# Second layer of a two-layer transformer with expert networks: the chosen experts' output bias, fetched per token by indirect transfers and added on VectorE

## The chip, the cores and the metric

The kernel runs on 1 core of one Trainium2 chip. Its time is the device time of one execution in microseconds (us). Before the change the median of three runs is 465.22 us (464.97 to 474.35).

The engines are named as the profile names them: PE is TensorE (matrix products, with PEld for its weight loads), DVE is VectorE, ACT is ScalarE, POOL is GpSimd and SP is SyncE. PE writes its results to PSUM (`ps`), the other tiles lie in SBUF, and inputs and outputs in DRAM.

## What is computed

32 images become 50 tokens of 192 numbers each (49 patches and a class token). Two layers follow. Layer 0 is a gated linear recurrence and an expert network with two chosen experts out of eight. Layer 1 is an attention on complex queries and keys and a switch network, in which each token goes to one expert. The change lies in this last part:

```python
x_enc = xt @ enc_w + enc_b
route_prob = jax.nn.softmax(x_enc @ sw_w + sw_b, axis=-1)
route_prob_max = jnp.max(route_prob, axis=-1)
routes = jnp.argmax(route_prob, axis=-1)
onehot = jax.nn.one_hot(routes, E, dtype=xt.dtype)
h = jnp.einsum('td,edr->ter', xt, w1) + b1[None]
h = jax.nn.gelu(h, approximate=False)
h = h * onehot[..., None]
out = jnp.einsum('ter,erd->td', h, w2) + onehot @ b2
out = out * route_prob_max[:, None]
```

Here `xt` is the normed token, E is 8, and `b2` has a row of 192 numbers for each expert. The result is added to the token `h`.

## The kernel before

**Tiles and stages.** The 32 images are four chunks (`CHUNKS`) of eight images. A chunk holds 400 tokens as four tiles (`TILES`) of 128 rows, two images a tile, each image padded from 50 to 64 rows. Layer 0's attention part runs in pairs of tiles until about 115 us of the span, its experts in a loop over 32 expert tiles until about 270 us, and layer 1 fills the rest, some 185 us.

**Layer 1.** Every engine runs a list of instructions written out by hand. A loop over the chunk number c sets the order. Iteration c computes the attention of chunk c and, between its pieces, the switch network of chunk c-1. The switch network of chunk 3 stands behind the loop. On PE an iteration is: the transposes of chunk c-1 (`turn`, L674), then `scores` (L941) of the four tiles, with `encode` (L983), `switch_logits` (L991), `hidden` (L1007) and `turned_choice` (L999) of chunk c-1 in between; then the queries and keys of the next chunk (L909), then `outputs` of chunk c-1 (L1019, L1020), then `attention` (transposes of the weights L964, products L974), and the rest of the next chunk's queries, keys and values (L909, L920). In iteration 3 there is no next chunk: only half of `outputs(2)` stands ahead of `attention(3)`, the other half behind it, and then the transposes of chunk 3 (L1080) open the tail.

**The switch network's output.** `outputs(c, half)` multiplies, for each of two tiles, the hidden values `s_hidT` with `s_w2` in four products (L1019) and adds the bias in a fifth (L1020). The fifth one's operands are rows 96 to 103 of `xT[1]`, in which the one-hot choice of each token stands transposed, and `s_b2`, whose rows 0 to 95 are zero and whose rows 96 to 103 are `b2`. DVE then computes in `output(c, half)` (L1869 to L1885) `out_tok = ps * s_prob + h` for each tile. Its first part reduces the exponentials to `s_prob`; that waits for ACT's exponential (L1286), which ACT issues between the attention weights of tiles 0 and 1 (L1262).

**The choice.** `route(c)` on DVE (L1845 to L1867) reads the logits and makes `s_best` and `s_onehot`. It runs early in iteration c+1, behind the first tile's `add_squares` (L1787, L1790); `output(c, ...)` runs late in it, ahead of `context` (L1805, L1808, L1813, L1816), which scales the attention's result, adds it to `h` and takes the statistics. POOL computes the inverse deviations of the norms (`rooted`, L605 and L607), for which DVE waits before it writes the normed tokens (L1420, and L1832 for chunk 3). In the attention and expert parts of layer 0 POOL also issues indirect transfers: `scatter` (L623) and the stores of L649.

The functions in their own words:

## Time and profile before

| | |
|---|---|
| median of the runs | 465.22 us (464.97, 465.22, 474.35) |
| the profiled execution's time | 459.67 us |
| its span, first to last instruction | 457.9 us |
| PE busy | 417.6 us, 91% of the span |
| PEld busy | 366.1 us, 80% |
| DVE busy | 274.3 us, 60% |
| ACT busy | 204.0 us, 45% |
| POOL busy | 96.3 us, 21% |
| granted TensorE clock, mean | 0.976 |
| the chain that ended last, by engine | PE 71%, DVE 10%, ACT 7%, issue 4%, DMA 4%, POOL 2% |

The profile is of one execution. Busy times are sums over the span; engines overlap. The chain is followed back from the last instruction, at each step to what released it. In the timeline a row is an instruction or a run of like ones, with its start, its length and, in brackets, how long the engine had been idle and what ended that. A multiplication of 32-bit numbers on PE leaves two records for each product of the program, so that 16 bias products give 32 records. The granted clock is 1.00 (2.4 GHz) nearly everywhere in layer 1.

### The profile page before, as it was taken

What the parts mean: (1) busy time and instruction counts of PE and PEld (TensorE: products, weight loads), DVE (VectorE), ACT (ScalarE), POOL (GpSimd) and SP (SyncE); (2) the same over time, 40 slices, a digit from 0 to 9 for tenths busy, and PEclk for the clock granted to TensorE, in tenths of its full rate; (3) what the DMA queues carried; (4) which work ended last, traced back from release to release, by engine and by line L of the source; (5) the groups of instructions that cost most, each with busy time, mean ns of one, the idle gap of its engine ahead of it and who ended that gap; (6) DMA issues with size and microseconds to landing.
All of it is one profiled execution on the core that took longest, in us unless ns stands there. A gap on an engine that the chain in (4) does not pass through costs nothing.

```text
span 457.9 us, 11718 instructions
## 1 busy us (share of the span) xinstructions
PE 417.6 (91%) x3944; PEld 366.1 (80%) x3945; DVE 274.3 (60%) x992; ACT 204.0 (45%) x427; POOL 96.3 (21%) x139
## 2 busy tenths in 40 slices
PE   5999999987699999999999938988799999999986
PEld 5899999887599999999999937656559757777845
DVE  4478888876334544554554447977686673665621
ACT  1333334521134544543553431267585377368440
POOL 3113555555402113112212211110101100100100
PEclk9999999997699999999999988999999999999999
DMA  7899802411312112112212225200001000100010
GB/s 233 319 375 400 326 31 75 132 36 51 97 38 61 40 41 63 41 36 53 67 35 52 62 53 179 69 4 1 1 1 28 2 3 2 28 1 1 2 28 27
DMA packets 30082, 35.43 MB, mean 77 GB/s; under 512 B 9315, under 2 KB 25379, under 8 KB 30047
## 3 DMA queue, kind: packets, MB, share of 16 engines
q1 hardware_dynamic: 25115, 28.52, 19.5%
q0 software_dynamic: 3072, 4.95, 3.3%
q10 hardware_dynamic: 1860, 1.49, 1.1%
q8 instruction: 22, 0.36, 0.3%
q14 instruction: 13, 0.11, 0.1%
HBM read 27.19 MB, written 9.14 MB: 79 GB/s over the span
## 4 chain that ended last, share of the span: by engine, by line
PE 71%; DVE 10%; ACT 7%; issue 4%; DMA 4%; POOL 2%; SPq 1%; DVEq 1%; POOLq 0%; ACTq 0%
PE ps L883 13%; PE ps L851 8%; PE ps L698 7%; PE ps L909 6%; PE ps L1019 5%; PE ps L862 5%; PE ps L1007 4%; PE ps L941 2%; PE ps L974 2%; PE ps L742 2%; PE ps L964 2%; PE ps L752 1%; ACT squares L1249 1%; PE ps L983 1%; PE ps L920 1%
## 5 line engine op out<-in xcount | busy, mean ns | idle before, releaser
L883 PE MATMUL ps<-w,hidT 128*128 x384 | 65.1, 326 | 0.0
L883 PEld LDWEIGHTS ps<-w,hidT 128*128 128x128 f32 x384 | 62.0, 190 | 0.0
L649 POOL DMA_INDIRECT ys_dram<-ys,y_place_now x32 | 31.1, 972 | 117.3 <-DVE ys L1699 112.4
L1212 ACT ACTIVATE hidT<-ps,b_act_now 128x128 f32<-128x128 f32 x96 | 28.2, 364 | 51.5 <-issue 49.2
L851 PE MATMUL ps<-xsT,low_now 128*128 128x128 f32 x384 | 49.8, 280 | 0.1
L851 PEld LDWEIGHTS ps<-xsT,low_now 128*128 128x128 f32 x384 | 46.0, 191 | 2.4 <-ACT xsT L1188 0.4
L605 POOL TENSOR_TENSOR rstd<-meanvar,eps 128x2 f32<-128x2 f32 (+1 forms) x25 | 5.4, 216 | 187.5 <-DVE meanvar L1839 73.8
L1684 DVE TENSOR_SCALAR hidT<-ps,b_dve_now 128x128 f32<-128x128 f32 x96 | 27.7, 344 | 21.4 <-PE ps L862 21.4
L698 PE MATMUL ps<-w_tok,patches 128*128 128x192 f32 x192 | 36.0, 342 | 5.0 <-DMA patches<-in_patches 5.0
L685 PE MATMUL ps<-ident 128*128 128x128 f32 x164 | 27.5, 335 | 12.5 <-DMA y_first<-ys_dram 8.4
L623 POOL DMA_INDIRECT xs_dram<-x_tok,rows x32 | 32.0, 1001 | 28.0 <-DVE rows L1568 20.7
L698 PEld LDWEIGHTS ps<-w_tok,patches 128*128 128x128 f32 x192 | 33.5, 200 | 4.8 <-DMA patches<-in_patches 4.7
L685 PEld LDWEIGHTS ps<-ident 128*128 128x128 f32 x164 | 26.0, 246 | 13.3 <-issue 13.0
L1195 ACT COPY low_now<-w_low 128x768 f32 x34 | 28.3, 832 | 0.0
L862 PE MATMUL ps<-xsT,high_now 64*128 64x128 f32 x384 | 25.7, 280 | 0.0
L1007 PE MATMUL ps<-xT,s_w 96*128 96x400 f32 (+1 forms) x64 | 24.2, 512 | 1.6 <-ACT xT L1291 1.6
L1019 PE MATMUL ps<-s_w,s_hidT 128*128 128x192 f32 x128 | 23.9, 330 | 1.2 <-ACT s_hidT L1299 1.2
L862 PEld LDWEIGHTS ps<-xsT,high_now 64*128 64x128 f32 x384 | 22.7, 187 | 1.9
L1674 DVE COPY b_dve_now<-b 128x3 f32 x32 | 5.4, 169 | 30.5 <-DVE hidT L1684 27.0
L1019 PEld LDWEIGHTS ps<-s_w,s_hidT 128*128 128x128 f32 x128 | 21.0, 189 | 3.4 <-ACT s_hidT L1299 3.3
L1249 ACT ACTIVATE squares<-ps 128x1200 f32<-128x1200 f32 x16 | 18.7, 1171 | 9.4 <-PE ps L941 9.3
L1699 DVE TENSOR_TENSOR ys<-ps,b 128x192 f32<-128x192 f32 x32 | 11.4, 357 | 18.0 <-PE ps L883 9.9
(225 smaller groups left out, 787.8 us busy)
## 6 DMA issues: line engine op xcount, KB each, us to landing
patches<-in_patches SPq DMA_DIRECT2D x7, 768.0 KB, 7.7
w<-in_W SPq DMA_DIRECT2D x8, 576.0 KB, 11.9
xs<-xs_dram SPq DMA_DIRECT2D x36, 96.0 KB
w_low<-in_W_low SPq DMA_DIRECT2D x8, 384.0 KB, 11.1
w_high<-in_W_high SPq DMA_DIRECT2D x8, 192.0 KB, 11.3
y_first<-ys_dram SPq DMA_DIRECT2D x4, 384.0 KB, 3.7
y_second<-ys_dram SPq DMA_DIRECT2D x4, 384.0 KB, 4.4
xs<-xs_dram SPq DMA_DIRECT2D x36, 33.0 KB
```

The lines of the kernel that those rows point to most:

```text
L623: nc.gpsimd.indirect_dma_start(out=xs_dram[:, :], out_offset=bass.IndirectOffsetOnAxis(ap=rows[:, k, 2 * c + i:2 * c + i + 1], axis=0), in ...
L649: nc.gpsimd.indirect_dma_start(out=ys_dram[:, :], out_offset=bass.IndirectOffsetOnAxis(ap=y_place_now[v][:, 0:1], axis=0), in_=ys[v][:, :] ...
L685: pe.matmul(ps[:, bank, 0:P], ident[:, :], ident[:, :], start=True, stop=True)
L698: mm = pe.matmul(ps[:, c % 2, D * i:D * i + D], pair_of(patches, c)[:, i, k, :], w_tok[:, k, :], start=(k == 0), stop=(k == KC - 1))
L851: mm = pe.matmul(ps[:, 4 + 2 * v + m // 3, P * (m % 3):P * (m % 3) + P], low_now[v][:, P * m:P * m + P], xsT[v][:, 0, :], start=(starts an ...
L862: mm = pe.matmul(ps[:, 4 + 2 * v + half, P * j:P * j + P], high_now[v][rows_, P * j:P * j + P], xsT[v][rows_, 1, :], start=(starts and j = ...
L883: mm = pe.matmul(ps[:, 2 * v + 1, 0:D], hidT[v][:, m, :], w2[:, bass.ds(experts[v], 1), D * m:D * m + D].rearrange("p e n -> p (e n)"), st ...
L1007: mm = pe.matmul(ps[:, FFN[c][m], 0:CT], s_w1[0:k, g, P * m:P * m + P], seqs(xT[1][0:k, g, :]), start=(g == 0), stop=(g == 1))
L1019: pe.matmul(dst, s_hidT[:, m, P * i:P * i + P], s_w2[:, m, :], start=(m == 0), stop=False)
L1195: nc.scalar.copy(low_now[v][:, :], w1_low[:, bass.ds(e, 1), :].rearrange("p e n -> p (e n)")).then_inc(w1_act_done, 1)
L1212: last = nc.scalar.activation(hidT[v][:, m, :], ps[:, 4 + 2 * v, P * m:P * m + P], ACT.Relu, bias=b1_act_now[v][:, m:m + 1])
L1684: last = nc.vector.tensor_scalar(hidT[v][:, 3 + m, :], ps[:, 5 + 2 * v, P * m:P * m + P], b1_dve_now[v][:, m:m + 1], 0.0, ALU.add, ALU.max)
```

## The change

For chunks 0, 1 and 2 the fifth product (L1020) is left out, and the fourth one ends the accumulation. Chunk 3 keeps it. In its place:

- `route(c)` computes on DVE, behind `s_onehot`, the number of the bias row of each token, `bias_row = 104 - s_best`, as an integer (one instruction on 128x4).
- `load_biases(c)` on POOL waits for it (and for the previous use of the buffer) and issues four indirect transfers, one a tile. Each fetches for 128 tokens the row of 192 numbers (768 bytes) from the input `s_b2` in DRAM into the new tile `bias_tok`.
- `output(c, 0)` on DVE waits for the four transfers, computes `out_tok = bias_tok * s_prob + h` for all four tiles, waits for its own last write, and then adds `ps * s_prob` to `out_tok` where it used to add it to `h`.

```diff
--- before.py
+++ after.py
@@ -254,6 +254,8 @@
         s_rank = sb("s_rank", [P, TILES, E])
         s_best = sb("s_best", [P, TILES])
         s_onehot = sb("s_onehot", [P, TILES, E])
+        bias_row = sb("bias_row", [P, TILES], I32)
+        bias_tok = sb("bias_tok", [P, TILES, D])
 
 
 
@@ -353,6 +355,9 @@
         s_rank_done = sem("s_rank_done")
         s_best_done = sem("s_best_done")
         onehot_done = sem("onehot_done")
+        bias_row_done = sem("bias_row_done")
+        bias_in = sem("bias_in")
+        bias_added = sem("bias_added")
         onehotT_in_psum = sem("onehotT_in_psum")
         onehotT_done = sem("onehotT_done")
         s_hid_in_psum = sem("s_hid_in_psum")
@@ -656,10 +661,24 @@
 
                 for c in range(2):
                     inverse_deviation(2, c)
+                def load_biases(c):
+
+                    pool.wait_ge(bias_row_done, c + 1)
+                    if c:
+                        pool.wait_ge(bias_added, c)
+                    for i in range(TILES):
+                        nc.gpsimd.indirect_dma_start(
+                            out=bias_tok[:, i, :], out_offset=None, in_=A["s_b2"][:, :],
+                            in_offset=bass.IndirectOffsetOnAxis(ap=bias_row[:, i:i + 1], axis=0),
+                            bounds_check=FG + E - 1, oob_is_err=False).then_inc(bias_in, 16)
+
                 for c in range(CHUNKS - 1):
+                    if c:
+                        load_biases(c - 1)
                     if c + 2 < CHUNKS:
                         inverse_deviation(2, c + 2)
                     inverse_deviation(3, c)
+                load_biases(CHUNKS - 2)
                 for half in range(2):
                     of = slice(2 * half, 2 * half + 2)
                     rooted(meanvar[1][:, of, 1], rstd[1][:, of], CHUNKS + half, var_done[3], eps_added[3], rstd_done[3])
@@ -1016,9 +1035,11 @@
                     for i in range(2 * half, 2 * half + 2):
                         dst = tokv(4)[:, i // 2, i % 2, :]
                         for m in range(4):
-                            pe.matmul(dst, s_hidT[:, m, P * i:P * i + P], s_w2[:, m, :], start=(m == 0), stop=False)
-                        mm = pe.matmul(dst, xT[1][0:FG + E, 1, P * i:P * i + P], s_b2[:, :],
-                                       start=False, stop=True)
+                            mm = pe.matmul(dst, s_hidT[:, m, P * i:P * i + P], s_w2[:, m, :], start=(m == 0),
+                                           stop=(c < CHUNKS - 1 and m == 3))
+                        if c == CHUNKS - 1:
+                            mm = pe.matmul(dst, xT[1][0:FG + E, 1, P * i:P * i + P], s_b2[:, :],
+                                           start=False, stop=True)
                     mm.then_inc(s_out_in_psum, 1)
 
                 turn(2, 0, 0, 1)
@@ -1865,6 +1886,11 @@
                         dve.wait_ge(onehotT_in_psum, c)
                     nc.vector.tensor_tensor(s_onehot[:, :, :], s_rank[:, :, :], spread(s_best[:, :], E),
                                             ALU.is_equal).then_inc(onehot_done, 1)
+                    if n < CHUNKS:
+                        if c:
+                            dve.wait_ge(bias_in, 16 * TILES * c)
+                        nc.vector.tensor_scalar(bias_row[:, :], s_best[:, :], -1.0, float(FG + E), ALU.mult,
+                                                ALU.add).then_inc(bias_row_done, 1)
 
                 def output(c, half):
 
@@ -1876,11 +1902,19 @@
                         dve.wait_ge(s_prob_done, c + 1)
                         if c >= 2:
                             dve.wait_ge(out_done[c % 2], 32 * (c // 2))
+                        if c < CHUNKS - 1:
+                            dve.wait_ge(bias_in, 16 * TILES * (c + 1))
+                            for i in range(TILES):
+                                last = nc.vector.scalar_tensor_tensor(
+                                    out_tok[c % 2][:, i, :], bias_tok[:, i, :], s_prob[:, i:i + 1],
+                                    h_tile(c, i), ALU.mult, ALU.add)
+                            last.then_inc(bias_added, 1)
+                            dve.wait_ge(bias_added, c + 1)
                     dve.wait_ge(s_out_in_psum, 2 * c + half + 1)
                     for i in range(2 * half, 2 * half + 2):
                         last = nc.vector.scalar_tensor_tensor(
                             out_tok[c % 2][:, i, :], tokv(4)[:, i // 2, i % 2, :], s_prob[:, i:i + 1],
-                            h_tile(c, i), ALU.mult, ALU.add)
+                            out_tok[c % 2][:, i, :] if c < CHUNKS - 1 else h_tile(c, i), ALU.mult, ALU.add)
                     if half or c == CHUNKS - 1:
                         last.then_inc(out_ready, 1)
 
```

On PE, the end of iteration 3 and the switch network's output of chunks 2 and 3. `s_hidT`, `s_w_202`, `s_b_203` and `xT_86` are the tiles `s_hidT`, `s_w2`, `s_b2` and `xT[1]`. Before:

```order
L1019 MATMUL ps<-s_w_202,s_hidT 128x192 x4
L1020 MATMUL ps<-s_b_203,xT_86 128x192
L1019 MATMUL ps<-s_w_202,s_hidT 128x192 x4
L1020 MATMUL ps<-s_b_203,xT_86 128x192
L1080 MATMUL ps<-ident,x_tok_84 96x128 x8
L983 MATMUL ps<-xT_86,enc_w 64x400 x2
```

After:

```order
L1038 MATMUL ps<-s_w_202,s_hidT 128x192 x8
L1101 MATMUL ps<-ident,x_tok_84 96x128 x8
L1002 MATMUL ps<-xT_86,enc_w 64x400 x2
```

The bias products are gone, nothing took their place on PE, and the transposes of chunk 3 follow directly. The same holds for all twelve tiles of chunks 0 to 2.

On DVE, in iteration 2 of layer 1, from the output of chunk 1 to the first tile of the attention's result. `ctx_tok` is the scaled result of a tile. Before:

```order
L1873 TENSOR_REDUCE s_sum<-s_exp 128x4
L1875 RECIPROCAL s_prob<-s_sum 128x4
L1881 SCALAR_TENSOR_TENSOR out_tok_206<-ps,s_prob,h 128x192 x4
L1805 RECIPROCAL inv_sum_236<-ps 128x12
L1808 TENSOR_TENSOR ctx_tok_238<-ps,inv_sum_236 128x4x3x16
```

After:

```order
L1899 TENSOR_REDUCE s_sum<-s_exp 128x4
L1901 RECIPROCAL s_prob<-s_sum 128x4
L1908 SCALAR_TENSOR_TENSOR out_tok_206<-bias_tok,s_prob,h 128x192 x4
L1915 SCALAR_TENSOR_TENSOR out_tok_206<-ps,s_prob,out_tok_206 128x192 x4
L1826 RECIPROCAL inv_sum_236<-ps 128x12
L1829 TENSOR_TENSOR ctx_tok_238<-ps,inv_sum_236 128x4x3x16
```

Four instructions stand between `s_prob` and the first output, and `context` is behind them.

On POOL, from iteration 1 of layer 1 to its end, with the changed kernel's line numbers. `meanvar_75` and `rstd_79` belong to the norm ahead of the attention, `meanvar_76` and `rstd_80` to the one behind it.

```order
L670 DMA bias_tok<-in_s_b,bias_row 128x192 x4
L610 TENSOR_TENSOR rstd_79<-meanvar_75,eps 128x4
L612 TENSOR_TENSOR rstd_79<-rstd_79,neg_half 128x4
L610 TENSOR_TENSOR rstd_80<-meanvar_76,eps 128x4
L612 TENSOR_TENSOR rstd_80<-rstd_80,neg_half 128x4
L670 DMA bias_tok<-in_s_b,bias_row 128x192 x4
L610 TENSOR_TENSOR rstd_80<-meanvar_76,eps 128x4
L612 TENSOR_TENSOR rstd_80<-rstd_80,neg_half 128x4
L670 DMA bias_tok<-in_s_b,bias_row 128x192 x4
L610 TENSOR_TENSOR rstd_80<-meanvar_76,eps 128x2
L612 TENSOR_TENSOR rstd_80<-rstd_80,neg_half 128x2
```

Each group of four transfers now stands ahead of the inverse deviations that come later in its iteration.

## Rows read from the trace of the kernel before

**Rows 1.** Windows, iterations 1 and 3: length, busy us and records of each engine, clock
```profile
340.00:360.00 20.00, 19.54 (x180) 15.62 (x179) 14.35 (x50) 10.77 (x17) 2.41 (x4) 1.00 0.06 17
420.00:440.00 20.00, 18.90 (x192) 15.76 (x191) 8.54 (x30) 9.89 (x17) 1.84 (x4) 1.00 0.06 17
```

**Rows 2.** Chain that ended last, iteration 1, outputs of chunk 0: start, us, what
```profile
342.77 1.57 PE ps L1019 x8
344.34 0.33 PE ps L1020 x2
344.66 1.30 PE ps L1019 x8
...
349.22 0.33 PE ps L1020 x2
```

**Rows 3.** Timeline of DVE, iteration 1: start, us, instruction, idle before
```profile
330.94 0.19 DVE L1866 TENSOR_TENSOR s_onehot<-s_rank,s_best 128x32 f32<-128x32 f32 x1
...
334.19 0.78 DVE L1787 TENSOR_TENSOR sc<-squares 128x600 f32<-128x600 f32 x1 [0.86 <-ACT squares L1249]
...
347.73 0.18 DVE L1875 RECIPROCAL s_prob<-s_sum 128x4 f32<-128x4 f32 x1
347.94 0.74 DVE L1881 SCALAR_TENSOR_TENSOR out_tok<-ps,s_prob,h 128x192 f32<-128x192 f32 x2
...
352.03 0.23 DVE L1805 RECIPROCAL inv_sum<-ps 128x12 f32<-128x12 f32 x1 [1.71 <-PE ps L974]
...
353.66 0.23 DVE L1805 RECIPROCAL inv_sum<-ps 128x12 f32<-128x12 f32 x1 [0.22 <-PE ps L974]
```

**Rows 4.** Groups by line, DVE, 340 to 345 us: us of all, mean ns
```profile
L1738 DVE SCALAR_TENSOR_TENSOR h<-y_first,all_gates,h 128x192 f32<-128x192 f32 x4 | 1.4, 409 | 0.0
```

**Rows 5.** Timeline of DVE, iteration 2
```profile
370.68 0.19 DVE L1866 TENSOR_TENSOR s_onehot<-s_rank,s_best 128x32 f32<-128x32 f32 x1
...
385.33 0.18 DVE L1875 RECIPROCAL s_prob<-s_sum 128x4 f32<-128x4 f32 x1
...
391.78 0.23 DVE L1805 RECIPROCAL inv_sum<-ps 128x12 f32<-128x12 f32 x1 [1.71 <-PE ps L974]
```

**Rows 6.** Timeline of DVE, iteration 3
```profile
410.43 0.19 DVE L1866 TENSOR_TENSOR s_onehot<-s_rank,s_best 128x32 f32<-128x32 f32 x1
...
423.82 0.18 DVE L1875 RECIPROCAL s_prob<-s_sum 128x4 f32<-128x4 f32 x1
...
427.49 0.23 DVE L1805 RECIPROCAL inv_sum<-ps 128x12 f32<-128x12 f32 x1 [1.59 <-PE ps L974]
...
434.97 0.67 DVE L1832 TENSOR_SCALAR x_tok<-h,meanvar,rstd 128x192 f32<-128x192 f32 x2 [0.66 <-POOL rstd L607]
```

**Rows 7.** Timeline of ACT, iteration 3
```profile
423.47 1.88 ACT L1262 ACTIVATE sc<-sc 128x600 f32<-128x600 f32 x3
425.70 1.50 ACT L1270 COPY probsT<-ps 128x768 f32<-128x768 f32 x2 [0.35 <-PE ps L964]
```

**Rows 8.** Chain that ended last, iteration 3, transposes of chunk 3
```profile
435.11 0.91 PE ps L1080 x7
```

**Rows 9.** Line 623, POOL's indirect transfers of layer 0: ns and landing us, min/median/max
```profile
L623 POOL DMA_INDIRECT xs_dram<-x_tok,rows x32: 967/972/1213, 43.6 to 116.3; - x32
...
DMA to landing us min/median/max: 2.3/2.4/5.9
```

**Rows 10.** Timeline of POOL, layer 0
```profile
77.81 0.97 POOL L623 DMA_INDIRECT xs_dram<-x_tok,rows  x1 [0.30 <-issue]
```

**Rows 11.** DMA issues: KB each, median us to landing
```profile
w<-in_W SPq DMA_DIRECT2D x8, 576.0 KB, 11.9
```

**Rows 12.** Timeline of POOL, iteration 1: the two inverse deviations behind the first gathers
```profile
344.95 0.20 POOL L605 TENSOR_TENSOR rstd<-meanvar,eps 128x4 f32<-128x4 f32 x1 [21.63 <-DVE meanvar L1413]
```

**Rows 13.** Line 1467 on DVE, both inputs in SBUF: ns min/median/max
```profile
L1467 DVE TENSOR_TENSOR h_plus_x<-h_plus_x,x_tok x8: 529/546/600, 15.8 to 87.9; 128x384 f32<-128x384 f32 x8
```

**Rows 14.** Timeline of DVE, layer 0
```profile
77.79 0.60 DVE L1467 TENSOR_TENSOR h_plus_x<-h_plus_x,x_tok 128x384 f32<-128x384 f32 x1
```

## The prediction

> **What bounds the kernel now.** The windows come first: in two windows of 20 us that cover most of iterations 1 and 3 of layer 1, PE is busy 19.54 and 18.90 us, DVE 14.35 and 8.54, POOL 2.41 and 1.84, all at a granted clock of 1.00 [rows 1]. So PE sets the pace of this stage and POOL is nearly free. Then the chain of waits, to see whether the removed products lie on it: at the outputs of chunk 0 it is an unbroken run of PE, 1.30 us of L1019 and 0.33 us of L1020 in turn, for four tiles [rows 2]. The bias products are on the chain, and what they cost is their full length. Last the timelines of DVE and ACT around the same place, which show who is next when PE becomes shorter: DVE has waits of 1.71, 1.71 and 1.59 us in front of the first tile of the attention's result [rows 3, 5, 6], and ACT in iteration 3 has only 0.35 us in front of its copy of the first weights [rows 7].
>
> **What is removed: 12 bias products on PE.** Each takes 0.33 us (two records) [rows 2]. In iterations 1 and 2 four are taken out of an unbroken run: 4 x 0.33 = 1.3 us each. In iteration 3 two go ahead of the attention and two behind it, 0.66 + 0.66 us, but there two other engines are next:
> - Ahead of the attention. The copy of the first weights on ACT starts at 425.70 after a wait of 0.35 us, because ACT finishes the three exponentials of tiles 1 to 3 at 423.47 + 1.88 = 425.35 [rows 7]. ACT does not move with PE, so the start of this copy gains 0.35 us, or up to 0.45 us because the records of like ACT instructions overlap by some 0.1 us (three in 1.88 us). I take 0.4; 0.26 of the 0.66 is lost.
> - Behind the attention. From its second tile on DVE works without a pause: it ends with the normed tokens of tiles 2 and 3 at 434.97 + 0.67 = 435.64 [rows 6], and the transposes of chunk 3 end on the chain at 435.11 + 0.91 = 436.02 [rows 8]. This DVE chain is set off by the attention's second tile and so moves by 0.4 us only, to 435.24. The last tile's two transposes (of eight in 0.91 us, so about 0.25) with some 0.15 us of hand-over then end near 435.65. So nothing of the second 0.66 us arrives, and PE waits instead, some 0.6 us. Iteration 3 gives 0.4 us in all.
>
> Sum of the gains: 1.3 + 1.3 + 0.4 = 3.0 us, out of the 3.9 us of PE time removed.
>
> **What is added on POOL: 12 gathers.** The trace has no gather from DRAM into SBUF. The nearest rows are the indirect transfers of layer 0, also 128 rows of about this size: 0.97 us of POOL each and 0.30 us between two, so four take 3 x 1.27 + 0.97 = 4.8 us, and they land 2.4 us after the issue, at worst 5.9 [rows 9, 10]. The upper bound of a landing is the slowest row of any issue, 11.9 us [rows 11]; the lower one is 2.3. I take 2.4. Then the fourth gather is there 7.2 us after the row numbers. Row numbers at the end of `s_onehot` plus 0.2 us for the new small instruction: 331.3, 371.1 and 410.8. Needed when `s_prob` is done: 347.9, 385.5 and 424.0 [rows 3, 5, 6]. Spare: 9.4, 7.2 and 6.0 us. The gathers cost nothing as long as this cover holds. Queued behind them on POOL are the inverse deviations. In iteration 1 the first is asked for at 344.95 [rows 12], and POOL is free at 336.1. In iterations 2 and 3 they come later still, behind `context`. SP's queue is not passed. The 512 rows of a chunk are 0.4 MB, for a DMA that moves 17 GB/s here [rows 1].
>
> **What is added on DVE.** Per chunk one small instruction behind `s_onehot`, 0.2 us like its neighbours. It pushes the second `add_squares` by 0.2 us, and the wait of 0.86 us on ACT that follows takes it up [rows 3]; without that cover it would cost 0.6 us in all. Then four instructions on 128x192. The nearest row is the same instruction with all tensors in SBUF, four in 1.4 us [rows 4]. With the wait for its own write (0.05 us, taken as the gap between other dependent DVE instructions of rows 3) it is 1.45 us. Without cover that would be 4.35 us in all, which is more than the PE time removed. The cover is DVE's wait ahead of `context`, and it must hold although PE comes earlier:
> - Iteration 1: start 347.94, bias until 349.4, four outputs (two in 0.74 us, four in 1.4) until 350.8. The attention's first tile is there at 352.03 - 1.3 = 350.7. DVE is 0.1 us late, and the wait of 0.22 us in front of the next tile absorbs it [rows 3].
> - Iteration 2: start 385.5, bias until 387.0, the last outputs follow PE until some 388.8; needed at 391.78 - 1.3 = 390.5 [rows 5].
> - Iteration 3: start 424.0, bias until 425.5, two outputs until 426.2; needed at 427.49 - 0.4 = 427.1 [rows 6].
>
> So DVE costs 0 to 0.1 us. The sum stays 3.0 us. The profiled execution has a span of 457.9 us and a time of 459.67 us. It would become 454.9 and 456.7. The median of the runs shown lies 5.5 us above the profiled execution; the same 3.0 us off it gives 465.2 - 3.0 = 462.2 us.
>
> **A rule that speaks against the change.** When an indirect transfer ran beside a DVE instruction with two inputs in SBUF, POOL's part kept its 0.97 us and DVE's took 0.60 us where the median of its line is 0.546 [rows 10, 13, 14]. So I charge nothing for it; at 0.05 us for each of some five DVE instructions beside the gathers it is 0.25 us an iteration, under the waits of 0.86 us. The Trainium skill, SBUF — State Buffer, section "Who interferes with whom", says otherwise: a DVE instruction with two SBUF inputs and a GpSimd instruction that reads SBUF exclude each other for their whole length, and the one that starts second is held. By that rule the gathers and DVE's `add_squares` and shifts, which have both inputs in SBUF, would hold each other; this is the third rival.
>
> **Rivals.**
> 1. *The last iteration gives its whole 1.3 us* (0.08). For it: the chain passes PE there. Against: the two waits above of 0.35 and 0.66 us. It gives 465.2 - 3.9 = 461.3.
> 2. *The gathers come late; slower than before* (0.07). All 512 fetches of a chunk read the same eight rows of DRAM, which nothing in this trace does. Place: DVE's wait in `output(c, 0)`, with `context` queued behind it and PE's last attention products behind that. In iteration 3 it bites when the landing exceeds 2.4 + 6.0 + 0.9 = 9.3 us, in iteration 2 from about 11.7, in iteration 1 from about 11.8, and it decides the sign from about 12.3. At 12.5 the second tile of iteration 3 is 2.5 us later than before, iteration 2 keeps a gain of about 1.0 and iteration 1 of 0.7: +0.8, 466.0. At 16 us it would be some 11 us slower, over 2%.
> 3. *POOL and DVE hold each other; slower than before* (0.07). Beside four gathers of 0.97 us DVE runs some five long instructions. If each gather held DVE for its length, that is 3.9 us an iteration, less the wait of 0.86: 3.0, three times 9.1, less the gain of 3.0: 465.2 + 6.1 = 471.3. Half of it would be 466.8. Against: rows 13 and 14, which show 0.05.
> 4. *DVE is late for `context`* (0.10). If the added instructions or the wait for the own write cost 0.3 us more than taken, iteration 1 uses up its wait of 0.22 and passes the rest on, some 0.2 us, and iteration 3 is near its limit too; if the misjudgement is 1 us, about 0.8 us is lost: 463.
>
> **How the numbers follow.** The forecast has 0.68, its own range from 461.3 to 463.2 us. The rivals' 0.08, 0.07, 0.07 and 0.10 make it 1.00. The range takes in rivals 1 and 4 and the near end of 2, and below that the level of the runs themselves: the profiled execution of the same kernel was 5.5 us under the median, so a median that falls in between is possible. That gives 459.0 to 466.0. Only rival 3 and the far end of 2 are left out, and the runs' own scatter. Over 2% (9.3 us, about what a measurement of this kernel can tell from no change) faster needs more than twice the PE time that is removed: 0.01. Over 2% slower needs the far end of rival 2, or 2 and 3 together (6.1 us alone is 1.3%): 0.03. Within 2%: 0.96.
>
> **What would show it.** In the changed profile: 12 fewer bias products (24 records), iteration pitch on PE shorter by 1.3, 1.3 and 0.4 us; the gathers of 0.97 us with landings near 2.4 us, 6 us ahead of their use; `s_prob` followed at once by the four additions in about 1.4 us; `context` in iteration 1 with no wait in front of its first tile; in iteration 3 ACT's copy with no wait in front, and the transposes L1101 now waiting some 0.6 us for DVE's `x_tok`. Wrong it would be if DVE waits for `bias_tok`, if the `sc` instructions beside the gathers are longer than 0.8 us, or if the clock falls below 1.00 in layer 1.

## The result and the profile after

The changed kernel takes 486.06 us (483.24 to 492.27, six runs) where the kernel before takes 465.1 us (461.49 to 474.35, six runs): 1.046 times as long, interval 1.0384 to 1.0537. It is 21 us slower, and the forecast was 3 us faster. The profiled execution took 485.37 us; its span is 483.6 us. Any kernel has executions that are some per cent slower at a lower clock; ratios leave these out, so a ratio can differ a little from the quotient of two medians.

The chip matters in this case, so each run below is told with the number of its chip (that of the first measurement is not known). The page of the kernel before shows a chip of one kind, the page after one of another: line 1233 (ACT's `hidT` in layer 0's experts; line 1212 before) waits 53.3 us in all for "issue" after, and 49.2 us before, although the change does not touch it. DVE's first sum of layer 1 (line 1738 before, 1759 after) starts at 281.10 instead of 275.65. These 5.5 us lie ahead of everything that was changed. What the change does is therefore read from the stage itself, from one `s_onehot` to the next; this distance is called the pitch of an iteration (start us, us, instruction):

```profile
338.12 0.19 DVE L1887 TENSOR_TENSOR s_onehot<-s_rank,s_best 128x32 f32<-128x32 f32 x1
...
383.65 0.19 DVE L1887 TENSOR_TENSOR s_onehot<-s_rank,s_best 128x32 f32<-128x32 f32 x1
...
429.83 0.19 DVE L1887 TENSOR_TENSOR s_onehot<-s_rank,s_best 128x32 f32<-128x32 f32 x1
...
466.98 0.19 DVE L1887 TENSOR_TENSOR s_onehot<-s_rank,s_best 128x32 f32<-128x32 f32 x1
```

The pitches are 45.53, 46.18 and 37.15 us. Before, by [rows 3, 5, 6] and a fourth `s_onehot` at 441.46, they are 39.74, 39.75 and 31.03. So the three iterations are 5.8, 6.4 and 6.1 us longer, where they should be 1.3, 1.3 and 0.4 us shorter. The two profiled spans differ by 25.7 us: 18.3 us of it is in these iterations, 7.2 us is ahead of the first `s_onehot`, where no gather has run yet, and 0.2 us is behind the last one.

The waits of ACT after, by engine, line and releaser: us in all, times, longest. The line that is new is the one of `squares`:

```profile
ACT hidT L1233 <- issue: 53.3, 15, 4.5
...
ACT squares L1270 <- remote: 16.5, 3, 5.5
```

Three waits, one an iteration, together 16.5 us. "Remote" means that no work of this core's engines that the profile knows of ended just then. The timelines of POOL, PE and ACT at the first of them:

```profile
339.27 1.11 POOL L670 DMA_INDIRECT bias_tok<-in_s_b,bias_row  x1 [10.29 <-DVE bias_row L1892]
...
343.31 1.00 POOL L670 DMA_INDIRECT bias_tok<-in_s_b,bias_row  x1 [0.30 <-issue]
```

```profile
339.23 0.98 PE L960 MATMUL ps<-kk,q 32*64 32x100 f32 x46
...
340.54 0.38 PE L960 MATMUL ps<-kk,q 32*64 32x100 f32 x2 [0.33 <-issue]
...
340.85 1.12 PE L1018 MATMUL ps<-ident,s_onehot 128*8 128x128 f32 x8
...
346.18 1.14 PE L960 MATMUL ps<-kk,q 32*64 32x100 f32 x40 [4.21 <-ACT squares L1270]
```

```profile
338.72 0.72 ACT L1277 ACTIVATE sc<-sc 128x612 f32<-128x612 f32 x1
...
344.96 1.17 ACT L1270 ACTIVATE squares<-ps 128x1200 f32<-128x1200 f32 x1 [5.52 <-remote]
```

The score products of the third tile (line 960) have all started by 340.92, and those of `turned_choice` behind them (line 1018) by 341.97. ACT is free and waits for just these scores, but is let go only at 344.96. That is 0.65 us after the last of the four gathers has ended (343.31 + 1.00). The other two iterations show the same: 390.44 against 389.73, and 436.61 against 435.93. PE shows a trace of it earlier: in all three iterations its 48 score products have a gap of 0.33 to 0.38 us after the 45th or 46th, at about the end of the first gather (e3 and e5 have none). At the first place this gap ends at 340.54 us, and the first packet that carries gathered rows starts at 341.09. So the delay begins before any row is moved. PE cannot go on without ACT and idles for 4.21 us. The clock falls after that; windows of the same place (length, busy of PE, PEld, DVE, ACT, POOL, granted clock, DMA share, GB/s):

```profile
338.00:340.90 2.90, 2.57 (x53) 1.41 (x52) 2.51 (x6) 1.42 (x2) 1.33 (x2) 1.00 0.03 6
340.90:344.90 4.00, 1.07 (x9) 0.50 (x8) 0.00 (x0) 0.00 (x0) 2.80 (x3) 1.00 0.32 74
344.90:350.00 5.10, 3.82 (x52) 2.52 (x53) 3.43 (x5) 4.12 (x5) 0.00 (x0) 0.53 0.09 19
```

### The profile page after: what moved, and what is told of

Read it like the earlier page. It is cut to its first block, busy times and chain, and to the rows that moved or that the text cites. A ratio compares the mean times of both kernels' runs of the same rounds, so it can differ in the third digit from the quotient of the medians.

```text
span 483.6 us, 11714 instructions
## 1 busy us (share of the span) xinstructions
PE 429.5 (89%) x3920; PEld 369.7 (76%) x3921; DVE 278.8 (58%) x1007; ACT 203.9 (42%) x427; POOL 109.3 (23%) x151
## 4 chain that ended last, share of the span: by engine, by line
PE 72%; DVE 6%; ACT 6%; issue 4%; DMA 3%; another core or an unknown queue 3%; POOL 2%; SPq 1%; DVEq 1%; POOLq 0%; ACTq 0%
PE ps L902 11%; PE ps L870 8%; PE ps L717 7%; PE ps L928 6%; PE ps L1026 4%; PE ps L881 4%; PE ps L1038 4%; PE ps L704 4%; PE ps L960 3%; PE ps L761 2%; PE ps L771 2%; PE ps L993 2%; PE ps L748 2%; PE ps L740 2%
## 5 line engine op out<-in xcount | busy, mean ns | idle before, releaser
L1233 ACT ACTIVATE hidT<-ps,b_act_now 128x128 f32<-128x128 f32 x96 | 28.2, 364 | 55.6 <-issue 53.3
L704 PE MATMUL ps<-ident 128*128 128x128 f32 x164 | 28.5, 344 | 13.0 <-DMA y_first<-ys_dram 8.5
L704 PEld LDWEIGHTS ps<-ident 128*128 128x128 f32 x164 | 27.1, 255 | 13.7 <-issue 13.4
L1026 PE MATMUL ps<-xT,s_w 96*128 96x400 f32 (+1 forms) x64 | 31.4, 637 | 0.7 <-ACT xT L1312 0.7
L960 PE MATMUL ps<-kk,q 32*64 32x100 f32 x768 | 17.1, 289 | 14.7 <-ACT squares L1270 12.7
L960 PEld LDWEIGHTS ps<-kk,q 32*64 32x64 f32 x768 | 13.1, 150 | 22.2 <-ACT squares L1270 15.1
L1270 ACT ACTIVATE squares<-ps 128x1200 f32<-128x1200 f32 x16 | 18.7, 1171 | 24.8 <-remote 16.5
L1808 DVE TENSOR_TENSOR sc<-squares 128x600 f32<-128x600 f32 x16 | 12.5, 783 | 28.3 <-ACT squares L1270 28.3
L881 PE MATMUL ps<-xsT,high_now 64*128 64x128 f32 x384 | 25.7, 280 | 0.0
L1026 PEld LDWEIGHTS ps<-xT,s_w 96*128 96x128 f32 (+1 forms) x64 | 14.5, 242 | 11.4 <-issue 6.2
```

What stands on the lines that cost most here:

```text
L704: pe.matmul(ps[:, bank, 0:P], ident[:, :], ident[:, :], start=True, stop=True)
L881: mm = pe.matmul(ps[:, 4 + 2 * v + half, P * j:P * j + P], high_now[v][rows_, P * j:P * j + P], xsT[v][rows_, 1, :], start=(starts and j = ...
L960: mm = pe.matmul(ps[HALF * b:HALF * b + HALF, r, HW * j:HW * j + HW], q[32 * r:32 * r + 32, j, P * i + HALF * b:P * i + HALF * b + HALF], ...
L1026: mm = pe.matmul(ps[:, FFN[c][m], 0:CT], s_w1[0:k, g, P * m:P * m + P], seqs(xT[1][0:k, g, :]), start=(g == 0), stop=(g == 1))
L1233: last = nc.scalar.activation(hidT[v][:, m, :], ps[:, 4 + 2 * v, P * m:P * m + P], ACT.Relu, bias=b1_act_now[v][:, m:m + 1])
```

## The experiments

**The forecast's own sum, with the gathers left out (chip 4).** In `e1_adds_no_gathers` the twelve gathers are replaced by one increment and `bias_tok` is zero, so the bias of chunks 0 to 2 is missing:

```diff
-                    for i in range(TILES):
-                        nc.gpsimd.indirect_dma_start(... bias_tok[:, i, :] ...).then_inc(bias_in, 16)
+                    pool.sem_inc(bias_in, 16 * TILES)
```

> The four transfers of each chunk are left out (bias_tok is zero, so chunks 0 to 2 lack their output bias); the four additions on DVE stay, the 12 bias products stay removed. Theory G (the gathers cause the loss): about 3 us faster than before, 462, and no wait of ACT of over 1 us behind the scores of tile 1. Theory L (the loss lies in the longer DVE list or in the changed program itself): still above 475 us.

Measured: 457.98 us against 460.48 before, 0.9948 (0.9918 to 0.9978). Its four `s_onehot` start at 330.28, 368.70, 407.12 and 437.68: pitches of 38.42, 38.42 and 30.56 us, which is 1.32, 1.33 and 0.47 us less than before. The forecast said 1.3, 1.3 and 0.4. The PE and DVE part of the sum is right, iteration by iteration. As the next runs show, chip 4 has no loss with gathers either, so e1 alone does not show that the gathers make it.

**One gather a chunk, other rows, later gathers (chip 4).** `e2_one_gather` fetches tile 0 only (no bias for tiles 1 to 3). `e3_distinct_rows` fetches 128 different rows from another tensor, so the bias is replaced by other values:

```diff
-                            ... in_=A["s_b2"][:, :], ... ap=bias_row[:, i:i + 1] ...
+                            ... in_=ys_dram[:, :], ... ap=row_index_int[:, 0:1] ...
```

`e4_late_gathers` is the change with one more wait at the head of `load_biases`, which holds POOL until ACT has squared the scores of all four tiles:

```diff
                     pool.wait_ge(bias_row_done, c + 1)
+                    pool.wait_ge(squares_done, TILES * (c + 2))
```

> Only tile 0 of each chunk is gathered, tiles 1 to 3 get no bias. Theory A (PE's increment of scores is delivered only when POOL is through with its last gather): ACT's wait ends 0.7 us after the one gather, which is about when the scores are done anyway, so no stall and about 463 us. Theory S (the stall has a fixed cost, about 4 us each, whatever the number of gathers): ACT still waits 5.5 us, three times, and the time stays above 475.

> The same 12 gathers at the same place, but each fetches 128 different rows of ys_dram instead of eight rows of s_b2 (the bias of chunks 0 to 2 is replaced by those rows). Theory C (many reads of the same eight rows hold the memory path): the wait of 5.5 us shrinks below 2 us, about 465. Theory A: nothing changes, 486, three waits of 5.5 us.

> As the change, but POOL issues the gathers only when the four tiles of scores of the iteration are squared, so that they run beside the products of 96 and 128 rows. Theory B (the stall needs the score products of 32 rows in flight): no stall, 462 to 463 us. Theory A: whatever PE finishes next is delivered late, a stall of 3 to 4 us moves to hidden or the queries, still about 480.

Measured: 458.07, 457.81 and 458.63 us, that is 0.9971 (0.9946 to 0.9997), 0.9961 (0.9919 to 1.0004) and 0.997 (0.9931 to 1.0009). None of the three shows a wait of ACT's squares on "remote". That e3, with twelve gathers beside the score products, has none was against every theory so far. It could be the rows, or the chip. In e4 the pitches are 38.43, 38.43 and 30.56 us: the whole forecast gain is there.

**The change once more (chip 14).** `e5_change_again` is the changed kernel, word for word.

> The changed kernel once more, on the chip on which the next three run. If the stall belongs to the kernel: about 4 to 5% slower than before and three waits of ACT of 5.5 us. If it belonged to the chip or the session of the first measurement: about 458 us and no wait.

Measured: 457.39 us against 461.63, 0.9897 (0.9865 to 0.9929): here the change is 4.2 us faster (the three pitches account for 2.9 of it). The same gathers stand beside the same score products and nothing is held (timelines of PE and ACT):

```profile
333.95 1.01 PE L960 MATMUL ps<-kk,q 32*64 32x100 f32 x48
...
334.88 1.04 PE L1018 MATMUL ps<-ident,s_onehot 128*8 128x128 f32 x8
```

```profile
334.99 1.17 ACT L1270 ACTIVATE squares<-ps 128x1200 f32<-128x1200 f32 x1 [0.84 <-PE ps L960]
```

The pitches are 38.54, 38.48 and 30.62 us (`s_onehot` at 332.84, 371.38, 409.86 and 440.48). So the 21 us are not in the kernel alone; they need a certain kind of chip too. (No chip was used at two different times, so what is called a kind of chip here could also be a state that a chip is in for a while. It is not the loading of one program: four programs ran on chip 9 below, and the marks of the kind are in all four.)

**Parts of it on chip 14.** `e6_gathers_only` is the kernel before plus the gathers, whose rows nothing uses. `e7_same_rows_ys` reads by the repeated row numbers from `ys_dram`, and `e8_distinct_rows_b2` reads 128 different rows of `s_b2` as far as it has them; in both the bias is replaced.

> The kernel before with the row numbers and the 12 gathers of the change added, but nothing reads the gathered rows: all bias products stay on PE, the four additions on DVE are left out. If the gathers alone make the stall: before + 4 us of stall + the slow clock, three times, so 15 to 20 us slower. If the stall needs the shorter PE list or the additions: within 1 us of before.

> The gathers with the same row numbers (8 rows for 512 tokens) but from ys_dram instead of the input s_b2 (the bias of chunks 0 to 2 is replaced). Theory C (same rows): stall as in the change, 480. Theory T (the tensor s_b2 or its place in DRAM): no stall, 458.

> Gathers from s_b2 as in the change, but row p for partition p (104 different rows; partitions 104 to 127 are skipped; the bias of chunks 0 to 2 is replaced). Theory C: no stall, 458. Theory T: stall as in the change, 480.

Measured: 461.94, 457.03 and 456.54 us, ratios 1.0007 (0.9977 to 1.0038), 0.9925 (0.9885 to 0.9965) and 0.9894 (0.9861 to 0.9927). On such a chip twelve unused gathers cost nothing that can be measured. None of the three shows a hold, whatever the rows, so they do not tell the theories apart.

**A chip that shows the loss (chip 9).** Four kernels ran there: the change again, `e4`'s kernel again, the change with eight gathers a chunk in place of four, and the change with plain transfers from POOL's queue:

```diff
-                        nc.gpsimd.indirect_dma_start(... in_=A["s_b2"][:, :], ...).then_inc(bias_in, 16)
+                        nc.gpsimd.dma_start(bias_tok[:, i, :], ys_dram[P * i:P * i + P, :]).then_inc(bias_in, 16)
```

The last one, `e12_direct_pool`, replaces the bias by other values.

> The changed kernel a third time, on whatever chip this falls. Theory P (the loss of the first measurement belongs to a chip or a loading of the program): 457 to 459 us again on most chips, and where it is 480 or more, the loop over the expert tiles is slower as well (9.1 instead of 8.75 us a turn). Theory K (it belongs to the kernel, and the chip of the second measurement was the exception): 480 or more.

> The late gathers on the same chip as the change. In both theories, if this chip shows no stall: the same time as the change within 0.5%. If it shows the stall: 460 if the scores in flight are needed (theory B), 475 or more if not (theory A).

> Each gather of the change is issued twice, the second time into a tile that nobody reads: 8 per chunk. If the gathers press on PE or on its increments even where no stall is seen, the products beside them get longer and it is over 1 us slower than the change. By the working of the prediction the eight gathers end 10.5 us after the row numbers and land at 344.3, 384.1 and 423.8, just ahead of their use at 347.9, 385.5 and 424.0: no cost, same as the change within 0.5 us.

> The 12 gathers are replaced by 12 plain transfers of 128 rows from ys_dram, also issued by POOL (the bias of chunks 0 to 2 is replaced). No stall on this chip: same as the change. On a chip with the stall: it stays if any transfer of POOL's makes it, it goes if it needs the gather's form.

| kernel on chip 9 | us (before: 466.33) | ratio | pitches, us | ACT's squares on "remote" |
|---|---|---|---|---|
| e9, the change | 483.22 | 1.0384 (1.0294 to 1.0474) | 45.02, 46.18, 36.87 | 16.6 us, 3 times |
| e10, gathers later | 462.66 | 0.9914 (0.9883 to 0.9945) | 40.99, 38.43, 30.57 | none |
| e11, eight gathers | 496.75 | 1.0639 (1.0522 to 1.0756) | 49.08, 49.98, 40.40 | 16.6 us, 3 times |
| e12, plain transfers | 466.96 (459.43 to 471.8) | none: its four runs scatter too far | 38.43, 38.43, 30.57 | none |

The loss is back in e9, in the same three places and with the same lengths. e10 has the same gathers, the same additions and the same products on the same chip; only the time at which POOL starts is another, and the loss is gone. Its second and third pitch are the forecast's. That is the decisive pair: the cost lies in what the gathers stand beside, not in the gathers, the additions or the rows. Iteration 2 of both, in the order of time: first gather and ACT's squares in e9, then the same squares and the first gather in e10 (timelines of POOL and ACT):

```profile
382.35 1.07 POOL L670 DMA_INDIRECT bias_tok<-in_s_b,bias_row  x1 [11.97 <-DVE bias_row L1892]
388.11 1.17 ACT L1270 ACTIVATE squares<-ps 128x1200 f32<-128x1200 f32 x1 [5.53 <-remote]
```

```profile
380.24 1.17 ACT L1271 ACTIVATE squares<-ps 128x1200 f32<-128x1200 f32 x1 [0.73 <-PE ps L961]
...
384.67 1.07 POOL L671 DMA_INDIRECT bias_tok<-in_s_b,bias_row  x1 [17.36 <-issue]
```

The first pitch of e10 is 2.6 us above e12's because the clock was 0.50 from 330 to 340 us, before its first gather (346.32); the kernels e6, e13, e15 and e17 show a long first pitch (40.5 to 42.3 us) with a low clock there too, on other chips. e11 missed its expectation of no cost by 13.5 us.

e12 was on the same chip and its four transfers stand beside the same products, but they are through POOL sooner, and the signal comes while POOL is still at them:

```profile
334.20 2.28 POOL L670 DMA_DIRECT2D bias_tok<-ys_dram  x4 [8.19 <-DVE bias_row L1889]
```

```profile
335.67 1.17 ACT L1267 ACTIVATE squares<-ps 128x1200 f32<-128x1200 f32 x1 [0.73 <-PE ps L957]
```

So a transfer from POOL's queue is not enough. Whether it is the gather's form or its longer time on POOL (5.0 us for four instead of 2.3) is not separated.

Where the rest of the loss comes from is seen by setting e9's second iteration against e10's (46.18 - 38.43 = 7.75 us). The wait of ACT takes 5.5 us in place of the 0.84 us that e5 shows: 4.7. Then PE, at the lower clock, needs 4.37 us for six of the hidden products (line 1026), where a group of six takes 2.26 us at the full clock (page after, ahead of the stall): 2.1. The next score products take 1.31 instead of 1.00 us: 0.3. That makes 7.1; 0.7 us is not assigned.

e11 shows that the products themselves are delayed, not only their signals. With eight gathers the next group of score products meets gathers too (timelines of PE and of POOL):

```profile
344.26 0.96 PE L966 MATMUL ps<-kk,q 32*64 32x100 f32 x28 [4.25 <-issue]
345.86 0.61 PE L966 MATMUL ps<-kk,q 32*64 32x100 f32 x4 [0.63 <-issue]
347.28 0.49 PE L966 MATMUL ps<-kk,q 32*64 32x100 f32 x3 [0.82 <-issue]
348.00 0.32 PE L966 MATMUL ps<-kk,q 32*64 32x100 f32 x1 [0.23 <-issue]
348.71 0.68 PE L966 MATMUL ps<-kk,q 32*64 32x100 f32 x12 [0.39 <-issue]
```

```profile
343.91 0.99 POOL L676 DMA_INDIRECT bias_spare<-in_s_b,bias_row  x1 [0.30 <-issue]
345.21 1.00 POOL L676 DMA_INDIRECT bias_spare<-in_s_b,bias_row  x1 [0.30 <-issue]
346.51 1.00 POOL L676 DMA_INDIRECT bias_spare<-in_s_b,bias_row  x1 [0.31 <-issue]
```

48 products that take 0.9 to 1.3 us elsewhere are strung out over 5.1 us, and the last twelve run on freely only 1.2 us after the last gather has ended (347.51). Twelve more gathers make the three pitches 4.06, 3.80 and 3.53 us longer, 0.95 us a gather. One detail speaks against the simplest form of the theory: in e11, too, ACT is let go for the first time at 343.04, 0.73 us after the fourth gather (342.31), although four more follow. The hold does not simply last until the gathers are over. PE's gaps here are put down to "issue": the trace names nothing that PE waited for, so a late supply of its instructions is not ruled out either.

The release has one more regularity that the theories above leave out. In all twelve holds (the page after, e9, e11 and, below, e18) ACT starts 5.67 to 5.77 us after the first gather of the group has begun, and 0.65 to 0.76 us after the fourth has ended. Four gathers always take about 5.0 us on POOL, so these two readings cannot be told apart, but with eight gathers the first hold is no longer. A hold of fixed length that the first gather starts (rival D of e15, below) therefore fits as well as one that the fourth gather ends.

**Alone, one gather, repeated rows: a third chip without the loss (chip 5).** Four runs were meant to tell what in the gathers does it.

> The kernel before with the twelve gathers added; nothing reads what they bring, the bias products stay and there are no additions. A chip that can show the loss is told by ACT's waits for s_hidT's source in the expert loop ('hidT <- issue'): 52.4 to 53.7 us in the five runs of such chips, 48.4 to 49.4 us in the others. Theory A (gathers beside the score products hold back PE's increments, and nothing else of the change is needed): on such a chip three waits of ACT's squares of about 5.5 us and 16 to 21 us over the kernel before, ratio about 1.04; on another chip 1.00. Rival B (the loss needs the shorter outputs or the additions of the change): no such wait and ratio 1.00 on either kind of chip.

> The change, with each gather reading 128 different rows of another DRAM tensor by a fixed list of rows, so the bias in chunks 0 to 2 is replaced by other values. Theory H1 (repetition of eight DRAM rows makes the gathers hold PE): no wait of ACT's squares over 3 us, ratio about 0.99. Theory H2 (any gather beside the score products does it): three waits of about 5.5 us and ratio about 1.04 on a chip whose expert loop shows 52 us or more of 'hidT <- issue'.

> The change with the gather of tile 0 alone; tiles 1 to 3 have zero bias in chunks 0 to 2. In the runs with the loss ACT's squares start 0.65 to 0.75 us after the fourth gather of a chunk ends, with four or with eight gathers. Theory C (the increments come 0.7 us after the gathers beside the score products end): one gather ends before the score products do, so no wait over 1.5 us and ratio about 0.99. Rival D (one gather is enough to start a fixed hold of some 5.5 us): the three waits stay at 5 us or more, ratio about 1.04. Between them, a price per gather of about 1.3 us would give waits of about 1.5 to 2 us.

> The change with the same lists of repeated rows, read from another DRAM tensor (written by the device) in place of the weight's; the bias in chunks 0 to 2 is replaced. Theory H1 (repetition): three waits of about 5.5 us as in the change, ratio about 1.04, while e14 shows none. Theory H3 (it is the input tensor s_b2 that matters): none here and none in e14. Theory H2 (any gather): waits of 5.5 us in both.

Measured: 460.61, 457.72, 458.02 and 456.77 us against 460.94; ratios 0.9995 (0.9956 to 1.0034), 0.9924 (0.9885 to 0.9964), 0.9945 (0.9896 to 0.9994) and 0.9897 (0.9864 to 0.993). ACT waits 48.7 to 49.7 us for "issue" at line 1233, which marks a chip without the loss, and no run shows a hold. So they tell nothing between the theories; rival D among them stays untested.

**Different rows on a chip with the loss.** The same kernel ran twice more. `e17` came to chip 11, of the kind without the loss: 457.11 us, 0.9937 (0.9908 to 0.9965), 48.9 us at line 1233. `e18` came to chip 8.

> As e14, on whatever chip comes: the change with each gather reading 128 different rows of another DRAM tensor, so the bias in chunks 0 to 2 is replaced. If the expert loop shows 52 us or more of 'hidT <- issue' (a chip of the kind that can show the loss): theory H1 (repetition of eight rows is needed) gives no wait of ACT's squares over 3 us and a ratio of about 0.99; theory H2 (any gather beside the score products) gives three waits of about 5.5 us and about 1.04. If it shows 48 to 50 us the run says nothing between them: no stall and about 0.99.

> The kernel of e17 on whatever chip comes (bias in chunks 0 to 2 replaced). If the expert loop shows 52 us or more of 'hidT <- issue': theory H1 (repetition of eight rows is needed) gives no wait of ACT's squares over 3 us and a ratio of about 0.99; theory H2 (any gather beside the score products) gives three waits of about 5.5 us and about 1.04. At 48 to 50 us the run leaves the question open.

e18 measured 483.96 us, ratio 1.0395 (1.0223 to 1.0566). The kernel before took 463.38 and 466.17 us there in the two runs that the ratio uses (471.06 us is the median of all five). With three runs against two the size of the loss is uncertain; the hold is not. Its waits of ACT:

```profile
ACT hidT L1233 <- issue: 52.1, 15, 3.8
...
ACT squares L1270 <- remote: 17.1, 3, 6.3
```

Here every gather reads 128 different rows of another tensor, and the hold is there all the same. So it needs neither the eight repeated rows nor the weight's tensor; theory H2 stands, for this kind of chip. At the first place PE reached the score products 1.9 us after the gathers had begun, and ACT was again let go 0.69 us after the fourth one had ended. Its wait of 6.28 us there is longer because PE was late, at a clock of 0.50 until about 340 us (timelines of PE, POOL and ACT):

```profile
340.61 1.16 PE L960 MATMUL ps<-kk,q 32*64 32x100 f32 x48
```

```profile
342.73 1.00 POOL L670 DMA_INDIRECT bias_tok<-ys_dram,row_index_int  x1 [0.30 <-issue]
```

```profile
344.42 1.17 ACT L1270 ACTIVATE squares<-ps 128x1200 f32<-128x1200 f32 x1 [6.28 <-remote]
```

## Why the prediction was wrong

**What held.** The removed products were worth what was said: pitches 1.32, 1.33 and 0.47 us shorter in e1, 1.20, 1.27 and 0.41 in e5. The details stand in e5 as forecast. `context` starts in iteration 1 without a wait (352.74, right behind the additions). ACT's copy in iteration 3 starts without one, and the transposes of line 1101 wait 0.51 us for `x_tok`. The four additions cost what was said, in the slow execution as well (timeline of DVE after, iteration 1):

```profile
362.26 1.41 DVE L1908 SCALAR_TENSOR_TENSOR out_tok<-bias_tok,s_prob,h 128x192 f32<-128x192 f32 x4
363.70 1.39 DVE L1915 SCALAR_TENSOR_TENSOR out_tok<-ps,s_prob,out_tok 128x192 f32<-128x192 f32 x4
365.01 0.23 DVE L1826 RECIPROCAL inv_sum<-ps 128x12 f32<-128x12 f32 x1
```

A gather takes POOL 1.00 to 1.11 us in the page after (up to 1.30 in e10) instead of 0.97, with the same 0.30 us between two. It lands after 3.2 to 3.3 us (the medians of e4 and e2) instead of 2.4; with different rows it is 2.8 us (e8 and e14), so reading the same rows costs some 0.4 us a landing. Neither matters: DVE waits nowhere for `bias_tok` in the page after.

**What failed.** The step is the sentence "The gathers cost nothing as long as this cover holds". It looked for their price in three places: at POOL, at DVE beside them, and at the reader of the rows. It did not look at PE, and so put what a gather does to PE's products and signals at nothing. The profile had no gather, and its indirect transfers stand in layer 0, beside wide products; no row shows any transfer from POOL beside the 32-row score products. So the cost of an unseen pair was set to zero and given no upper end, although PE was the engine that sets the pace. The runs showed in its place, on this kind of chip, three holds of ACT's squares of 5.5 us each with PE idle behind them, and a lower clock after each. Twelve gathers there cost 7.1, 7.8 and 6.6 us (the pitches of the page after against e12's 38.43, 38.43 and 30.57), 21.4 us in all.

**The rivals.** None was the cause. Rival 1 (a whole 1.3 us in the last iteration) is refuted by 0.47 and 0.41. Rival 2 (gathers too late) is refuted: the rows are there in time, and repeated rows are neither needed for the loss (e18) nor enough (e5). Rival 3 (POOL and DVE hold each other) came near in size and sign, but names the wrong engine: beside the gathers DVE's `sc` instructions of line 1808 take 777 to 786 ns, the same as everywhere. Rival 4 (DVE late for `context`) would have cost 0.2 us and more in iteration 1, which in e5 keeps 1.20 of the 1.3 us. The rule of the Trainium skill behind rival 3 (SBUF — State Buffer, "Who interferes with whom"), that the two exclude each other for a whole instruction, shows in no run here. The same section also says that `tensor_tensor` did not stall DMAs in its own probe, which agrees with these 777 to 786 ns and speaks against the use that the prediction made of the rule. What does show is smaller: the third and fourth gather of a group take 1.14 to 1.20 us in e5, beside DVE's `sc` instructions, and 1.00 to 1.01 us in the page after, where DVE is idle. Of the three signs of error that the prediction named, one came true: the clock fell below 1.00 in layer 1 (0.53 behind the stall). Behind the holds it is a consequence, worth 2.4 of some 7 us a time. Nor is it a sign of the gathers: in e10 the clock was 0.50 before the first gather.

**The level.** The prediction saw that the median shown lay 5.5 us above the profiled execution, and only widened its range for it. It may have been a sign. The kernel before takes 460.48, 461.63, 460.94 and 460.65 us on chips 4, 14, 5 and 11, and 466.33 us on chip 9; on chip 8 its five runs go from 463.38 to 474.15. By the marks in the trace the profile before was of the first kind and the profile after of the second. The times alone separate the kinds badly: single runs on chip 4 reach 466.3 us.

**Left open.** Two things. First, what makes these chips different: this is a sorting by signs that go together, not a cause, and no chip was tried a second time. Second, what path is shared. e11 shows that products and signals of PE are delayed beside gathers, and e10 that the pitch loses nothing when gathers run beside the wide products; whether it is the width of the products, their number in short time or their 32-row tiles was not tried. Nor did the kernels with one gather a chunk (e2, e15) or with gathers only (e6, e13) come to such a chip, so whether one gather is enough, and whether the shorter `outputs` and the additions play a part, is open.

## What to carry to other kernels

A transfer that is moved to an idle queue is not free because its reader can wait: name what the pacing engine does at that very time, and if no row shows the pair, give the term an upper end. When it may wait, put it beside work that is known to bear it: one line that holds POOL until the last scores are squared turned 1.0384 into 0.9914 on chip 9. It gave 0.997 (0.9931 to 1.0009) on chip 4, which is no proven gain in time there, though no kernel with gathers has shorter pitches. `e4`'s and `e10`'s kernel is the best correct one on the chip that punishes the change (462.66 us against 466.33 before and 483.22 for the change). And repeat a surprising loss on another chip before explaining it: chip 14 alone would have shown this change as a gain of 1%, chip 9 alone as a loss of 4%.

## What was not expected of the hardware

- On some chips POOL's gathers delay PE's score products and the signals that they are done: three waits of 5.5 us where other chips show 0.84 us, with 128x192 gathers of 1.0 us each. Plain transfers of the same size from the same queue (0.54 to 0.65 us each on POOL, landing 2.3 us) caused no such wait on chip 9.
- The kind of chip shows in a run that has no gathers beside scores at all. ACT's waits for "issue" at line 1233 are 52.1 to 53.7 us on chips 8 and 9 and in the page after, and 48.4 to 49.7 us elsewhere. DVE's first sum of layer 1 starts at 278.3 to 281.1 us there and at 273.0 to 277.8 us elsewhere, which is the weakest of the marks. And the trace holds 3,879 to 3,983 separate semaphore events there, against 5,235 to 5,433. Most of the missing ones are increments by transfers: the gathers' own semaphore has 118 events in e9 and 192 in e5. Whether increments arrive together or are only recorded together is not shown.
- The hold does not wait for the gathered rows. At the first place of the page after the rows' first packet starts 1.8 us after the first gather, when PE has already had its gap, and the last one ends 1.3 us after ACT has been let go. In the holds of the page after, e9 and e11 the late signal comes within 0.1 us of an increment by a gather, but in e18 the nearest one is 0.5 to 0.6 us away, so the two do not simply travel together.
